# A six-layer attention and FFN stack in one kernel: a written order for each of the four tiles of a unit

## What is computed

```python
q, k, v = split(shift_tokens(x) @ Wqkv)          # 16 heads of 64
q = rotary(l2norm(q) * qs); k = rotary(l2norm(k) * ksc)
sim = q k^T * 8 over this window and the one before, masked
x = (softmax(sim) @ v) @ Wo + x
xn = layernorm(shift_tokens(x)) * g + b          # ffn_layer
x = (a * gelu(gate)) @ W2 + b2 + x               # a, gate = split(xn @ W1 + b1)
```

## Time and profile before

| | us |
|---|---|
| median of three executions | 3657.97 |
| the profiled execution, its own time | 3635.34 |
| its span (first to last instruction) | 3633.5 |
| PE matmuls busy | 3380.5 (93%) |
| DVE busy | 2807.8 (77%) |
| POOL busy | 2818.6 (78%) |
| ACT busy | 2530.0 (70%) |

### The profile page before, as it was taken

One profiled execution on the slowest core, in us unless ns is written; L12 is line 12 of the kernel. 1 busy time (PEld: TensorE's weight loads), 2 busy tenths in 40 slices (PEclk: granted clock), 3 DMA queues, 4 the chain that ended last, 5 costly groups with the idle time before them and its releaser, 6 DMA issues.

```text
span 3633.5 us, 148686 instructions
## 1 busy us (share of the span) xinstructions
PE 3380.5 (93%) x64228; PEld 2686.8 (74%) x64228; DVE 2807.8 (77%) x4876; ACT 2530.0 (70%) x4686; POOL 2818.6 (78%) x3470
## 2 busy tenths in 40 slices
PE   3799986999999999999999999999999999999997
PEld 2566543788878888777888787887888877878775
DVE  3487666888888888888888888888888888888873
ACT  3333223778777888787887787887878877878763
POOL 1455546998888888888888888888888887888872
PEclk9899997999999999999999999999999999999998
DMA  3323211211111111111111121111111111111110
GB/s 101 105 92 94 86 33 54 55 42 41 46 48 49 42 43 43 47 44 47 44 39 46 49 52 39 43 43 50 46 47 41 42 44 49 39 43 47 36 43 24
DMA packets 126733, 183.46 MB, mean 50 GB/s; under 512 B 29824, under 2 KB 61440, under 8 KB 126080
## 3 DMA queue, kind: packets, MB, share of 16 engines
q1 hardware_dynamic: 119232, 146.15, 15.9%
q0 software_dynamic: 6848, 27.80, 2.4%
HBM read 59.01 MB, written 14.16 MB: 20 GB/s over the span
## 4 chain that ended last, share of the span: by engine, by line
PE 72%; POOL 8%; ACT 7%; issue 5%; DVE 4%; DMA 1%; SPq 0%; POOLq 0%; ACTq 0%; DVEq 0%
PE bank L548 17%; PE bank L611 9%; PE bank L622 8%; PE bank L584 7%; PE bank L558 5%; PE bank L595 4%; PE bank L685 3%; PE bank L663 3%; PE bank L674 3%; ACT big L1364 2%; ACT sq L1338 2%; PE bank L568 2%; POOL S L1686 1%; PE bank L523 1%; PE bank L463 1%
## 5 line engine op out<-in xcount | busy, mean ns | idle before, releaser
L548 PE MATMUL bank<-wqkv,xs 128*128 128x512 f32 x3456 | 1057.7, 422 | 19.3 <-DVE m L1017 13.6
L1678 POOL TENSOR_TENSOR m<-m 128x512 f32<-128x512 f32 x576 | 729.2, 1286 | 30.4 <-DVE m L1017 27.8
L548 PEld LDWEIGHTS bank<-wqkv,xs 128*128 128x128 f32 x3456 | 583.9, 191 | 103.7 <-issue 12.8
L1338 ACT ACTIVATE sq<-bank 128x512 f32<-128x512 f32 x768 | 458.9, 597 | 92.4 <-PE bank L548 54.5
L1017 DVE TENSOR_TENSOR m<-bank,tab 128x512 f32<-128x512 f32 x768 | 521.9, 680 | 0.3 <-POOL m L1678 0.3
L1686 POOL TENSOR_TENSOR S<-S,nw 128x1024 f32<-128x1024 f32 x192 | 383.4, 1997 | 172.9 <-DVE S L1048 172.9
L1028 DVE TENSOR_REDUCE ss<-sq 128x8 f32<-128x512 f32 x768 | 505.2, 675 | 0.0
L1694 POOL TENSOR_TENSOR S<-S,rs 128x512 f32<-128x512 f32 x384 | 411.6, 1093 | 52.9 <-DVE rs L1062 50.4
L611 PEld LDWEIGHTS bank<-P,big 64*64 64x64 f32 x24576 | 382.2, 136 | 79.9 <-issue 72.8
L1015 DVE TENSOR_TENSOR m<-bank,tab 128x512 f32<-128x512 f32 x576 | 392.5, 682 | 62.5 <-ACT sq L1338 47.1
L611 PE MATMUL bank<-P,big 64*64 64x32 f32 x24576 | 404.9, 221 | 3.5 <-issue 2.7
(11 more groups left out here) (229 smaller groups left out, 6628.5 us busy)
## 6 DMA issues: line engine op xcount, KB each, us to landing
big<-vst SPq DMA_DIRECT2D x1536, 64.0 KB, 2.0
stage<-in_wqkv SPq DMA_DIRECT2D x36, 256.0 KB, 2.9
tab<-in_tab SPq DMA_DIRECT2D x48, 128.0 KB, 2.2
xsort<-big SPq DMA_DIRECT2D x4, 960.0 KB, 8.9
big<-xsort SPq DMA_DIRECT2D x12, 256.0 KB, 6.3
ysort<-big SPq DMA_DIRECT2D x12, 256.0 KB, 3.6
wo<-in_wo SPq DMA_DIRECT2D x6, 512.0 KB, 3.5
big<-in_x SPq DMA_DIRECT2D x8, 256.0 KB, 3.4
```

Of the source, the lines that this page charges most:

```text
L548: m = eng.matmul(pb[:, :], xt[a], wqkv[:, z, 512 * part:512 * part + 512], start=(n == 0), stop=(n == 2))
L1338: eng.activation(sq[:, part % 2, :], bank[part % 2][:, :], ACT.Square, scale=1.0, bias=0.0).then_inc(s["a_sq"], 1)
L1678: eng.tensor_tensor(turned(g, part), turned(g, part), m2[:, part % 2, :], ALU.add).then_inc(s["g_add"], 1)
```

## The change

In the loops of PE, DVE, ACT and POOL the one order with conditions on q4 becomes four written orders, one for each q4. Some steps of a tile slide into the iteration before or after (an index n + 1 or n - 1 shows it). The functions, their waits, the banks, the buffers and SP's stream are the same, and so is the number of instructions. ACT starts with `high(1)` as well. After the loops a few calls follow that the loop no longer makes, and loops over f are written out (left out below, where nothing else changes). The lines stand 12 columns to the left.

```diff
--- before.py
+++ after.py
@@ -719,48 +719,88 @@
 
 for n in range(NG + 2):
     q4, u = n % 4, n // 4
-    proj(n, 0)
-    probs(n - 4, 0)
-    proj(n, 1)
-    probs(n - 4, 1)
-    out_proj(n - 5)
-    if q4 == 3:
-        down(u - 4)
-    if q4 == 2:
+    if q4 == 0:
+        end_variance(u - 6)
+        turn_q(n - 1, 0)
+        turn_q(n - 1, 1)
+        proj(n, 0)
+        probs(n - 4, 0)
+        proj(n, 1)
+        probs(n - 4, 1)
+        out_proj(n - 5)
+        proj(n, 4)
+        values(n - 4)
+        proj(n, 2)
+        turn_k(n - 2, 0)
+        proj(n, 3)
+        turn_k(n - 2, 1)
+        proj(n, 5)
+        sim(n - 2)
+        turn_q(n, 0)
+        turn_q(n, 1)
+        proj(n + 1, 0)
+        probs(n - 3, 0)
+        proj(n + 1, 1)
+        probs(n - 3, 1)
+        out_proj(n - 4)
+    elif q4 == 1:
+        gate(u - 4, 0)
+        values(n - 4)
+        gate(u - 4, 1)
+        proj(n, 4)
+        proj(n, 2)
+        turn_k(n - 2, 0)
+        turn_k(n - 2, 1)
+        proj(n, 3)
+        proj(n, 5)
+        gate(u - 4, 2)
+        sim(n - 2)
+        turn_q(n, 0)
+        proj(n + 1, 0)
+        turn_q(n, 1)
+        probs(n - 3, 0)
+        proj(n + 1, 1)
+    elif q4 == 2:
+        probs(n - 4, 1)
+        out_proj(n - 5)
         up(u - 4, 0)
         up(u - 4, 1)
-    if q4 == 1:
-        gate(u - 4, 0)
-        gate(u - 4, 1)
-    if q4 == 3:
+        values(n - 4)
+        proj(n, 4)
+        up(u - 4, 2)
+        proj(n, 2)
+        spread(u - 3)
+        turn_k(n - 2, 0)
+        proj(n, 3)
+        turn_k(n - 2, 1)
+        proj(n, 5)
+        end_spread(u - 6)
+        sim(n - 2)
+    else:
+        turn_q(n - 1, 0)
+        proj(n, 0)
+        turn_q(n - 1, 1)
+        probs(n - 4, 0)
+        proj(n, 1)
+        probs(n - 4, 1)
+        out_proj(n - 5)
+        down(u - 4)
         centre(u - 2)
+        values(n - 4)
         end_centre(u - 5)
-    values(n - 4)
-    proj(n, 4)
-    if q4 == 2:
-        up(u - 4, 2)
-    proj(n, 2)
-    if q4 == 2:
-        spread(u - 3)
-        end_spread(u - 6)
-    turn_k(n - 2, 0)
-    proj(n, 3)
-    turn_k(n - 2, 1)
-    proj(n, 5)
-    if q4 == 3:
+        proj(n, 4)
+        proj(n, 2)
+        turn_k(n - 2, 0)
+        turn_k(n - 2, 1)
+        proj(n, 3)
+        proj(n, 5)
         variance(u - 2)
-        end_variance(u - 5)
-    if q4 == 1:
-        gate(u - 4, 2)
-    sim(n - 2)
-    turn_q(n, 0)
-    turn_q(n, 1)
-end_spread(NU - 6)
-spread(NU - 3)
+        sim(n - 2)
 for par in range(2):
     vacant[4 + par] = [("v_sm", 2 * (NG - 1) + par + 1)]
     vacant[6 + par] = [("a_oev", 2 * NG)]
-probs(NG - 2, 0)
+end_spread(NU - 6)
+spread(NU - 3)
 probs(NG - 2, 1)
 out_proj(NG - 3)
 up(NU - 4, 0)
...
@@ -1147,43 +1189,78 @@
 low(0)
 for n in range(NG + 2):
     q4, u = n % 4, n // 4
-    reduced(n - 1, 3)
-    largest(n - 3)
-    lessened(n - 3)
-    weights(n - 1, 4)
-    weights(n - 1, 5)
-    if q4 == 3:
+    if q4 == 0:
+        reduced(n - 1, 1)
+        rotate(n - 1, 2)
+        rotate(n - 1, 3)
+        reduced(n - 1, 2)
+        norm_step(u - 3)
+        reduced(n - 1, 3)
+        weights(n - 1, 2)
+        end_step(u - 6)
+        largest(n - 3)
+        xn_low(u - 4)
+        lessened(n - 3)
+        weights(n - 1, 3)
+        rotate(n, 0)
+        weights(n - 1, 4)
+        reduced(n, 0)
+        reduced(n, 1)
+        residual(n - 5)
+        rotate(n, 1)
+        weights(n - 1, 5)
+    elif q4 == 1:
+        summed(n - 4)
+        inverted(n - 4)
+        rotate(n - 1, 2)
+        rotate(n - 1, 3)
+        largest(n - 3)
+        lessened(n - 3)
+        reduced(n - 1, 2)
+        reduced(n - 1, 3)
+        reduced(n, 0)
+        rotate(n, 0)
+        residual(n - 5)
+        reduced(n, 1)
+        summed(n - 3)
+        rotate(n, 1)
+        inverted(n - 3)
+        reduced(n, 2)
+    elif q4 == 2:
+        rotate(n - 1, 2)
+        rotate(n - 1, 3)
+        largest(n - 3)
+        lessened(n - 3)
+        reduced(n - 1, 3)
+        rotate(n, 0)
+        residual(n - 5)
+        hidden(u - 4, 0)
+        hidden(u - 4, 1)
+        reduced(n, 0)
+        rotate(n, 1)
+        hidden(u - 4, 2)
+        reduced(n, 1)
+        normed(u - 3)
+        summed(n - 3)
+        rotate(n, 2)
+        ended(u - 6)
+        inverted(n - 3)
+        reduced(n, 2)
+        rotate(n, 3)
+        largest(n - 2)
+    else:
+        reduced(n - 1, 3)
         low(u + 1)
-    rotate(n, 0)
-    weights(n, 0)
-    reduced(n, 0)
-    residual(n - 5)
-    reduced(n, 1)
-    if q4 == 2:
-        hidden(u - 4, 0)
-    rotate(n, 1)
-    weights(n, 1)
-    if q4 == 2:
-        hidden(u - 4, 1)
-    if q4 == 3:
+        lessened(n - 3)
+        residual(n - 5)
+        rotate(n, 0)
+        reduced(n, 0)
+        rotate(n, 1)
         closed(u - 4)
-    summed(n - 3)
-    if q4 == 2:
-        hidden(u - 4, 2)
-    inverted(n - 3)
-    if q4 == 3:
-        xn_low(u - 3)
-    if q4 == 2:
-        normed(u - 3)
-        ended(u - 6)
-    rotate(n, 2)
-    rotate(n, 3)
-    reduced(n, 2)
-    if q4 == 3:
-        norm_step(u - 2)
-        end_step(u - 5)
-    weights(n, 2)
-    weights(n, 3)
+        weights(n, 0)
+        summed(n - 3)
+        inverted(n - 3)
+        weights(n, 1)
 ended(NU - 6)
 normed(NU - 3)
 largest(NG - 1)
...
@@ -1480,47 +1560,93 @@
     eng.activation(e_s, bank[close_home("centre", u)][:, :], ACT.Square, scale=1.0, bias=0.0).then_inc(s["a_e"], 1)
 
 high(0)
+high(1)
 for n in range(NG + 2):
     q4, u = n % 4, n // 4
-    out_turned(n - 5, 1)
-    if q4 == 2:
+    if q4 == 0:
+        turned_q(n - 1, 1)
+        probs(n - 4, 0)
+        weights(n - 1, 3)
+        square(n, 0)
+        probs(n - 4, 1)
+        weights(n - 1, 4)
+        square(n, 1)
+        masked(n - 2)
+        exps(n - 3)
+        weights(n - 1, 5)
+        v_out(n, 0)
+    elif q4 == 1:
+        turned_k(n - 3, 0)
+        square(n - 1, 2)
+        turned_k(n - 3, 1)
+        square(n - 1, 3)
+        v_out(n - 1, 1)
+        out_turned(n - 5, 0)
+        turned_q(n - 1, 0)
+        turned_q(n - 1, 1)
+        out_turned(n - 5, 1)
+        probs(n - 4, 0)
+        probs(n - 4, 1)
+        square(n, 0)
+        square(n, 1)
+        exps(n - 3)
+        gelu(u - 4, 0)
+        gelu(u - 4, 1)
+        v_out(n, 0)
+        square(n, 2)
+        turned_k(n - 2, 0)
+        turned_k(n - 2, 1)
+        masked(n - 2)
+    elif q4 == 2:
+        square(n - 1, 3)
+        v_out(n - 1, 1)
         gelu(u - 4, 2)
-    turned_q(n - 1, 0)
-    turned_q(n - 1, 1)
-    weights(n - 1, 4)
-    weights(n - 1, 5)
-    square(n, 0)
-    weights(n, 0)
-    probs(n - 4, 0)
-    square(n, 1)
-    weights(n, 1)
-    probs(n - 4, 1)
-    if q4 == 2:
+        out_turned(n - 5, 0)
+        out_turned(n - 5, 1)
+        turned_q(n - 1, 0)
+        square(n, 0)
+        turned_q(n - 1, 1)
+        probs(n - 4, 0)
+        probs(n - 4, 1)
+        masked(n - 2)
+        square(n, 1)
         shifted(u - 2)
-    if q4 == 3:
+        exps(n - 3)
+        v_out(n, 0)
+        square(n, 2)
+        turned_k(n - 2, 0)
+        turned_k(n - 2, 1)
+        out_turned(n - 4, 0)
+        v_out(n, 1)
+        square(n, 3)
+        out_turned(n - 4, 1)
+        turned_q(n, 0)
+        square(n + 1, 0)
+        turned_q(n, 1)
+        probs(n - 3, 0)
         scaled(u - 3)
-    if q4 == 0:
-        high(u + 1)
-    exps(n - 3)
-    if q4 == 1:
-        gelu(u - 4, 0)
-    if q4 == 3:
+    else:
+        probs(n - 4, 1)
         xn_high(u - 3)
-    if q4 == 1:
-        gelu(u - 4, 1)
-    if q4 == 3:
+        weights(n, 0)
+        square(n, 1)
+        weights(n, 1)
+        masked(n - 2)
+        exps(n - 3)
         centred(u - 2)
+        out_turned(n - 4, 0)
         end_centred(u - 5)
-    masked(n - 2)
-    v_out(n, 0)
-    square(n, 2)
-    turned_k(n - 2, 0)
-    square(n, 3)
-    turned_k(n - 2, 1)
-    out_turned(n - 4, 0)
-    weights(n, 2)
-    weights(n, 3)
-    v_out(n, 1)
+        v_out(n, 0)
+        square(n, 2)
+        turned_k(n - 2, 0)
+        turned_k(n - 2, 1)
+        square(n, 3)
+        weights(n, 2)
+        v_out(n, 1)
+        high(u + 2)
+        turned_q(n, 0)
+        out_turned(n - 4, 1)
+out_turned(NG - 3, 0)
 out_turned(NG - 3, 1)
 scaled(NU - 3)
 gelu(NU - 4, 2)
...
@@ -1704,18 +1832,52 @@
 tables(0)
 for n in range(NG + 2):
     q4, u = n % 4, n // 4
-    weighed(n - 3)
-    scale(n - 2, 0)
-    scale(n - 2, 1)
-    add(n, 0)
-    add(n, 1)
-    divide(n - 3, 0)
-    divide(n - 3, 1)
-    if q4 == 3:
+    if q4 == 0:
+        divide(n - 4, 0)
+        divide(n - 4, 1)
+        add(n - 1, 2)
+        add(n - 1, 3)
+        chain(n - 1)
+        weighed(n - 3)
+        scale(n - 2, 0)
+        scale(n - 2, 1)
+        add(n, 0)
+        add(n, 1)
+    elif q4 == 1:
+        divide(n - 4, 0)
+        divide(n - 4, 1)
         tables(u + 1)
-    add(n, 2)
-    add(n, 3)
-    chain(n)
+        add(n - 1, 2)
+        weighed(n - 3)
+        scale(n - 2, 0)
+        add(n - 1, 3)
```

(62 more changed lines are left out.)

## The result

| | before | after |
|---|---|---|
| median of the runs taken together, us | 3656.89 (4 runs) | 3593.66 (4 runs) |
| ratio, 95% interval | | 0.983 (0.9815 to 0.9846) |
| profiled execution, its own time | 3635.34 | 3587.5 |
| span of the profiled execution | 3633.5 | 3585.7 |
| first to last `sim` of the layers | 2924.3 | 2865.9 |

The kernel is 1.7% faster. On the 3657.97 of before that is 62 us. The two profiled executions show 48 us of it: the layers are 58.4 us shorter, but the untouched first part took 10 us longer in this execution of after (the first `proj` starts at 592.1, before at 582.2). Over the profiled executions of all kernels of this study the first `proj` starts between 578 and 598 us, so I read the layers by themselves.

What follows compares the result with a forecast made beforehand. PE's own work was taken to set the pace (487.7 of 500 us busy). Terms 19.2 + 5.8 + 16.5 = 41.5 us took the profiled 3635.3 to 3594, or 3616.5 us against the median of 3658.0; range 3586 to 3650.

Steps and rivals of the forecast that it cites:

- rival 1: Layer ends vanish altogether (31.6 us, not 16.5) and some issue stalls go too: 3591 us; chance 0.20.
- (a): Tiles q4 = 1 and 3: turn_k 1 ahead of proj 3 removes PE's 0.20 us wait in 96 tiles, 19.2 us.
- variance takes 0.78: Sign that the forecast is right: PE's step before variance takes 0.78 us, with the wait for turned k gone.
- The cover of 0.15: At turn_k 1, PE's 1.13 us of work against the 0.98 handover of bank 2 leaves 0.15 us to spare.
- Rival 2: Wait returns at bank 2 (ACT 0.35 late for turn_k 1), 3635 us, or at layer ends, 3633; chance 0.13.
- (b): Tile q4 = 0: proj(n, 4) between out_proj and values saves 0.12 us in 48 tiles, 5.8 us.
- rival 5: By the tiling rule, moving proj(n, 4) ahead of values gains nothing: 35.7 us in all, 3622; chance 0.07.
- (c): Five layer ends: ACT takes weight blocks 4 and 5 after square and probs; 3.3 us saved each, 16.5 us.
- the 3.0 for DVE's list: At each layer end PE waits 3.0 us at proj(32, 3) for DVE's 11.1 us of blocks and passes.
- (d): Issue stalls in sim, 28.1 us, left unchanged; bounds 14 us less or more.
- (e): Steps moved on ACT, DVE and POOL cost nothing while those engines keep 70 to 100 us idle in 500.
- Rival 3: DVE reaches the row sums too late for q4 = 2, so PE's probs wait: slower, e.g. 3693 us; chance 0.08.

Runs made afterwards that it cites:

- e6: The changed kernel with PE and ACT back to proj 3 ahead of turned k 1 for q4 = 1 and 3: 0.991 of the kernel before.
- e2: The kernel before with only turn_k 1 moved ahead of proj 3 on PE and turned k ahead of square 3 on ACT, q4 = 1 and 3: 0.9992.
- e3: The kernel before with only proj(n, 4) moved ahead of values for q4 = 0: 0.9958, 15 us faster.
- e5: The changed kernel with ACT taking the next layer's weight blocks 4 and 5 ahead of square(n, 0) again: 0.9905 of the kernel before.
- e7: The changed kernel with turn_k 1 ahead of proj 3 on PE for q4 = 0 too: 0.9831 of the kernel before.
- e8: PE and ACT as in the changed kernel, DVE and POOL as before (DVE's blocks 4 and 5 moved): 1.005 of the kernel before, 18 us slower.
- e4: The kernel before with three edits only (weight blocks 4 and 5 later, turn_k 1 before proj 3, proj 4 before values): 0.991, 33 us faster.

## Why the prediction was right, and where it was not

The time by ratio (62 us less, some 3596) lies in the range and nearer to rival 1 (3591) than to the forecast (3616.5), though not by rival 1's reasons: the ends did not vanish. The direction was right, and the gain was 1.5 times the 41.5 that I had summed.

**(a) The size of the wait.** I took 0.20, the difference of 0.98 and a proj of 0.78. But the proj no longer ends alone. A proj followed by a proj takes 0.70, so two that follow each other save more: the step before `variance` or a gate went from 0.98 to 0.70, and what follows from 0.98 to 0.88 and from 0.86 to 0.78. Against that stand 0.08 for the first turned k, which now has another one behind it (0.44 for 0.36). Net 0.30 and 0.28 a tile, 28 us for 96 and 29 measured (e6, known to about 9), where the forecast had 19.2. The sign "variance takes 0.78" came as 0.70. The cover of 0.15 that I gave turned k 1 held in after, and in e2 too; there the loss came in the next tile, 0.5 us at proj 5. I had looked one bank ahead on PE; ACT's own list over the next tile is what I should have walked through too, from `exps` to turned k. Rival 2 named a late ACT, but at another bank (2, for turned k 1), in other tiles, and as something that the change itself would suffer; what happened was at bank 3 in the q4 = 0 tile, and only without the other engines' orders.

**(b) proj ahead of values: worth nothing.** The step that failed is "values costs nothing extra behind a matmul of 512 columns". The two gates before `values` take 1.55, where a pair of projs takes 1.49: 0.06 of the price was visible there, and I read it as nothing. The Trainium skill (TensorEngine Tiling (Array Packing), Key Properties) says that a change of tiling mode drains TensorE, with no exception for what stood before. The traces agree: 0.18 behind `out_proj`, 0.09 behind a single proj (0.87 for 0.78), and the q4 = 0 tile is unchanged. By that rule, which was rival 5, this term was to be 0. The 15 us that e3 measured all the same are not this term, and their source is open.

**(c) The layer ends: mechanism right, residue wrong.** The stall before `out_proj` left, as forecast. Its price was 7.2 an end (99.2 - 5 x 12.6 = 36.2 for five) where my rows summed to 6.3. The difference is the clock, which I had priced by the third end alone. In the 8 us behind the five stalls of before the granted clock is 0.66, 0.79, 0.79, 0.50 and 0.72; by the same sum that costs 12.3 us and not 8.0, and 23.6 + 12.3 = 35.9. And what remains in after is 74.0 - 5 x 12.53 = 11.4 for five, 2.3 each, for which I had 3.0. So 25 by the tiles and 27 by e5, in place of 16.5, and near the upper bound of 31.6. The low clock came with this stall and went with it (0.61 at the third end before, 0.50 at the first in e5, 1.00 at the first in after). The step that failed is the 3.0 for DVE's list: "PE would then wait 11.1 - 7.9 = 3.2 us". No wait of PE for DVE m stands in the list of after. At the first end DVE started the list 1.2 us before `proj(32, 0)` (1057.95 and 1059.16) and was through with it at 1067.14, after 9.2 us and not 11.1, while PE came to `proj(32, 3)` only at 1067.79:

```profile
1066.46 0.68 DVE L1059 TENSOR_TENSOR m<-bank,tab 128x512 f32<-128x512 f32 x1
...
1067.79 0.94 PE L548 MATMUL bank<-wqkv,xs 128*128 128x512 f32 x3
```

Most of the 1.9 is the split: its three blocks took 0.74, 0.69 and 0.87 us here (median of 30 in after 0.74) and not the mean of 1.21, 1.3 us less (why is in the last section). What is left at the ends of after is something else. PE's timeline at the third, fourth and fifth end:

```profile
2026.03 0.59 PE L611 MATMUL bank<-P,big 64*64 64x32 f32 x25 [1.36 <-issue]
...
2509.02 0.43 PE L611 MATMUL bank<-P,big 64*64 64x32 f32 x12 [2.31 <-issue]
...
2993.27 0.88 PE L548 MATMUL bank<-wqkv,xs 128*128 128x512 f32 x3 [1.64 <-issue]
```

These three make 5.3 of the 11.4. Behind the last two the granted clock falls again, to 0.57 and 0.59 over 4 us, which costs 3.4 us more; at the fourth end:

```profile
2509.00:2513.00 4.00, 3.98 (x24) 3.25 (x25) 2.21 (x3) 1.46 (x3) 4.00 (x4) 0.57 0.28 66
```

The same stalls stand at the same three ends in e6 (1.0, 1.4 and 1.5) and e7 (0.8, 0.9 and 1.9), so they belong to the place and are not chance; what causes them is open. The first two ends have no such stall in `values` or proj and take 13.7, with one wait of 0.3 and 0.4 for the half of k that POOL scales.

**(d) Issue stalls.** Over all of PE's lines they are 42 us after and 38 before, so the 14 either way held. In `sim` they fell from 28.1 to 23.6, in `values` they rose from 2.0 to 7.3, of which 3.7 are the two at layer ends just shown.

**(e) The cover of the other engines.** "They cost nothing as long as these engines keep their 70 to 100 us of idle time" came out for the change and is wrong as a reason. From 2000 to 2500 ACT is idle for 106 us in e2, 105 in e8 and 90 in after, and it is late in the first two; POOL has the least, 61 in after and 73 in e8, and PE waits for it in e8. Idle time in a stretch is no cover for one step; the order decides whether it lies where PE needs it. Rival 3 (the row sums) did not come: POOL S holds PE once, for 0.2, and POOL's wait for the reciprocals halved.

The sum with what was measured: 29 (a) + 0 (b) + 27 (c) = 56 of 62 us. The two measured terms are each known to about 9, so the other 6 can't be told from nothing. The three terms of the forecast without the rest of the rewrite are e4, and it has 33 us, not 41.5: (c) is worth 21 alone, (a) nothing. What the sum as a whole had wrong is the zero for the rest of the rewrite, without which (a) is not there. That the time still came out in the range owes something to luck: (b) was too high, (a) and (c) too low.

## What to carry to other kernels

When PE is the bound, look for the next engine's wait behind each one removed: here 0.3 us removed in one tile uncovered 0.5 in the next. Follow the copying engine's list through to there, step by step, before the gain is counted; its idle share (106 us of 500 where it was late, 90 where it was not) does not tell. And price a step in the place where it will stand (first of a pair, last of a pair, ahead of a change of tile shape), for the same three matmuls took 0.70, 0.78 or 0.87. When an engine's order is rewritten, test it with the other engines' old orders too: here that turned 1.7% faster into 0.5% slower.
